# Mamba layers as a pipeline of token halves: the end of one item and the preparation of the next are issued between the scan chunks of the one in the middle

## The reference

```python
def rmsnorm(x, w, eps=1e-05):
    return x * jax.lax.rsqrt(jnp.mean(x * x, axis=-1, keepdims=True) + eps) * w
def mamba_block(x, ...):
    xm, res = jnp.split(x @ in_w.T + in_b, 2, axis=-1)
    xm = jax.nn.silu(causal_depthwise_conv(xm, conv_w) + conv_b)      # 4 taps over tokens
    x_dbl = xm @ xp_w.T
    delta = jax.nn.softplus(x_dbl[..., :64] @ dt_w.T + dt_b)
    Bm, Cm = x_dbl[..., 64:80], x_dbl[..., 80:]
    def step(h, ins):                                                 # scan over tokens
        d_t, B_t, C_t, u_t = ins
        h = h * jnp.exp(d_t[:, :, None] * A) + (d_t * u_t)[:, :, None] * B_t[:, None, :]
        return (h, jnp.einsum('bds,bs->bd', h, C_t))
    y = (ys + xm * D_ssm) * jax.nn.silu(res)
    return y @ out_w.T + out_b
x1 = x + mb(rmsnorm(x, norm1_w)); out2 = memory_attend(mb(rmsnorm(x1, norm2_w))); return x1 + out2
```

## Time and profile before

| | |
|---|---|
| median of three runs | 3658.72 us |
| the profiled execution, its time / span | 3660.78 us / 3659.0 us |
| busy: PE / DVE / ACT / POOL | 2742.5 / 2217.9 / 1904.8 / 1665.2 us |
| share of the span | 75% / 61% / 52% / 46% |
| granted TensorE clock, mean | 0.90 |
| chain that ended last: PE / POOL / DVE / issue / ACT | 41% / 30% / 11% / 8% / 7% |
| the four batches / what follows them | 38 to 2765 us / 2765 to 3659 us |

### The profile page before, as it was taken

The page is one execution under the profiler, slowest core; times in us unless marked ns, Lnnn a source line. Parts: engine busy times, 40 slices in busy tenths (PEclk is TensorE's granted clock), DMA queues, the critical chain, the costliest instruction groups (busy, mean ns, idle before and its releaser), DMA issues.

```text
span 3659.0 us, 44328 instructions
## 1 busy us (share of the span) xinstructions
PE 2742.5 (75%) x15274; PEld 2050.4 (56%) x15275; DVE 2217.9 (61%) x2787; ACT 1904.8 (52%) x3028; POOL 1665.2 (46%) x1723
## 2 busy tenths in 40 slices
PE   5787688877777896687688867777895299999910
PEld 2674576547647754674676547647754166666600
DVE  4894893468668645894893468678643033333347
ACT  5785781378678525785781378678531011111100
POOL 2792791039639602792791039639602501000060
PEclk9898899889989998898899889989996599999955
DMA  5110120001001100110110001001102212111031
GB/s 197 43 51 1 41 64 1 12 18 52 25 18 50 38 1 13 44 50 1 44 61 1 12 18 53 24 18 53 35 1 102 81 62 90 62 63 62 33 93 47
DMA packets 91235, 158.84 MB, mean 43 GB/s; under 512 B 14130, under 2 KB 39986, under 8 KB 91058
## 3 DMA queue, kind: packets, MB, share of 16 engines
q1 hardware_dynamic: 72338, 106.80, 9.4%
q0 software_dynamic: 15392, 47.99, 3.6%
q10 hardware_dynamic: 3328, 1.76, 0.2%
HBM read 118.36 MB, written 38.14 MB: 43 GB/s over the span
## 4 chain that ended last, share of the span: by engine, by line
PE 41%; POOL 30%; DVE 11%; issue 8%; ACT 7%; DMA 2%; another core or an unknown queue 1%; DVEq 0%; POOLq 0%; SPq 0%; ACTq 0%
POOL arena L597 25%; PE psD L926 13%; PE psD L1237 7%; PE psA L926 6%; POOL arena L582 4%; PE psD L1114 2%; PE psA L1089 2%; PE psD L1135 2%; DVE arena L1351 2%; PE psA L973 2%; PE psA L1228 1%; DVE arena L1349 1%; PE psA L920 1%; ACT arena L779 1%; DVE arena L1338 1%
## 5 line engine op out<-in xcount | busy, mean ns | idle before, releaser
L597 POOL TENSOR_TENSOR arena<-arena 128x512 f32<-128x512 f32 x1024 | 1091.2, 1092 | 10.7 <-POOL carry L593 0.5
L1012 PE MATMUL psD<-ident,arena 128*128 128x128 f32 x4096 | 651.6, 286 | 274.6 <-ACT arena L779 209.9
L1012 PEld LDWEIGHTS psD<-ident,arena 128*128 128x128 f32 x4096 | 479.1, 146 | 374.0 <-ACT arena L779 273.5
L786 ACT ACTIVATE arena<-arena,negA 128x512 f32<-128x512 f32 x1024 | 662.1, 712 | 12.2 <-DVE arena L1363 11.4
L1363 DVE TENSOR_TENSOR_SCAN arena<-arena,psD 128x512 f32<-128x512 f32 x512 | 581.7, 1200 | 137.8 <-PE psA L1032 81.4
L1032 PE MATMUL psA<-ident,arena 128*128 128x128 f32 x4096 | 617.7, 274 | 19.0 <-POOL arena L597 18.7
L1363 DVE TENSOR_TENSOR_SCAN arena<-arena,carry,psD 128x512 f32<-128x512 f32 x512 | 602.4, 1255 | 37.0 <-PE psA L1032 37.0
L779 ACT ACTIVATE arena<-arena,bc 128x512 f32<-128x512 f32 x768 | 498.0, 712 | 87.4 <-PE psD L1012 86.3
L1032 PEld LDWEIGHTS psA<-ident,arena 128*128 128x128 f32 x4096 | 479.1, 142 | 32.3 <-POOL arena L597 32.3
L926 PE MATMUL psD<-arena 128*128 128x512 f32 (+4 forms) x776 | 336.9, 569 | 43.5 <-POOL strip L545 28.7
L883 ACT ACTIVATE in_w_sb<-in_w_sb 128x512 f32<-128x512 f32 x140 | 88.1, 630 | 457.6 <-DVE in_w_sb L1559 457.6
(11 more groups left out here) (202 smaller groups left out, 3527.6 us busy)
## 6 DMA issues: line engine op xcount, KB each, us to landing
arena<-c_dram SPq DMA_DIRECT2D x256, 256.0 KB, 3.2
arena<-in_W POOLq DMA_DIRECT2D x16, 1024.0 KB, 7.5
xs_dram<-zeros SPq DMA_DIRECT2D x40, 256.0 KB, 6.5
arena<-xs_dram SPq DMA_DIRECT2D x71, 128.0 KB
ys_dram<-arena POOLq DMA_DIRECT2D x70, 128.0 KB, 2.0
arena<-in_x SPq DMA_DIRECT2D x4, 1024.0 KB, 7.0
arena<-in_b POOLq DMA_DIRECT2D x8, 512.0 KB, 7.9
out<-arena SPq DMA_DIRECT2D x4, 1024.0 KB
```

The lines of the kernel that those rows point to most:

```text
L597: pool.tensor_tensor(h_ring[:, r % H_SLOTS, :], h_ring[:, r % H_SLOTS, :], c_rows[:, (half * NS + n) % C_SLOTS, :], ALU.mult).then_inc(c_w ...
L786: act.activation(da_ring[:, r % DA_SLOTS, :], dt[:, f, half * HALF:(half + 1) * HALF], ACT.Exp, scale=negA[:, f, n:n + 1]).then_inc(da_rea ...
L1012: mm = pe.transpose(psD[:, r % RING, j * P:(j + 1) * P], g[:, (r // KI) % 2, j, f * P:(f + 1) * P], ident[:, :])
```

## The change

A layer is no longer prepared for 1024 tokens at once. The four items of a batch are layer 0 first half, layer 0 second half, layer 1 first half, layer 1 second half. They form one scan run of 256 chunks a batch (`RUN = ITEMS * CHUNKS`). Every engine walks the steps c = -64 .. 256 + 19. `when(c)` gives the place r within a window of 64 chunks, and the items k (ending), s (being scanned) and p (being prepared). A table of constants says at which r each piece is issued; the piece comes after that step's regular work on its queue. The run's chunks are as wide as before.

- Two banks of psD take fills, the other two take all side work, under new semaphores (`bg_full`, `bg_by_act`, `bg_by_dve`). The decay ring has six slots instead of eight.
- Softplus runs block by block, and its functions alternate with the decays. The root is exp(-0.5 ln(mean + eps)) on ACT; before it was Sqrt on ACT and a reciprocal on DVE. POOL normalises. All tests for small exponentials are on POOL.
- The convolution carries its last three tokens from the first to the second half of a layer (`pads`).
- The output bias is added to x in place by POOL, layer 0 adds into xin, and x is read again from DRAM into base at the end of the batch for the final sum.
- The first part of x2 is read back after the last layer norm of the last batch; before, it was read after layer 0 of that batch.
- Zeros are written to DRAM in pieces twice as wide.

The diff, cut to its core. The constants and the two helpers:

```diff
-        RUN = 2 * CHUNKS
-        DA_SLOTS = H_SLOTS = 8
-        C_SLOTS = 4
+        ITEMS = 4
+        RUN = ITEMS * CHUNKS
+        TAIL = 20
+        DA_SLOTS, H_SLOTS, C_SLOTS = 6, 8, 4
+        FILL_BANKS = 2
         FILL_AHEAD, SUM_AFTER, DECAY_AHEAD, WEIGH_AFTER = 2, 6, 4, 4
...
+        TURN = [8, 10, 12, 14]
+        MO = [10, 12, 14, 16]
+        XNT = [22, 23]
+        IN = [25, 27, 29, 31]
+        GATE = [26, 28, 30, 32]
+        XD = [38]
+        BCT = [40]
+        Z = [41, 42, 43, 44]
+        UT = [50, 51, 52, 53]
+        KEEP_Y = 6
+        PADS, XB = 2, 1
+        SQUARE = [MO[j] + 2 for j in range(JT)]
+        RMS, NORM = 19, 20
+        SILU = 36
+        SOFT = [z + 2 for z in Z]
...
+        def when(c):
+            s, r = divmod(c, CHUNKS)
+            items = [q if 0 <= q < ITEMS else None for q in (s - 1, s, s + 1)]
+            return (r, *items)
```

SP:

```diff
+                for v in range(ITEMS * NS):
+                    q, n = divmod(v, NS)
+                    i = b * ITEMS + q
+                    if n == NS - 2 and q + 1 < ITEMS:
+                        store_c(i + 1)
...
+                sp.wait_ge(bg_by_dve, taken("turn", b * ITEMS + ITEMS - 1, JT - 1))
+                sp.dma_start(base, x[b].rearrange("(t p) d -> p t d", p=P)).then_inc(x_again, 16)
...
+            sp.wait_ge(ln_done, B * 2 * TT)
             sp.dma_start(x2[:, 0:TT, :], x2_dram[0:TT].rearrange("t p d -> p t d")).then_inc(x2_first, 16)
```

POOL:

```diff
+                def normalise(i):
...
+                    pool.wait_ge(inverse, 2 * (i + 1))
+                    for j in range(JT):
+                        pool.tensor_scalar(xn[:, j, :], xin[:, (i % 2) * JT + j, :],
+                                           inv_rms[:, 1, j:j + 1], 1.0, ALU.mult, ALU.mult).then_inc(normed, 1)
+                def soften(i, f):
+                    n = i * KI + f
+                    pool.wait_ge(soft_exp, n + 1)
+                    if n >= 2:
+                        pool.wait_ge(replaced, n - 1)
+                    pool.tensor_scalar(is_small[:, f % 2, :], soft_e[:, f, :], SMALL_E, None, ALU.is_lt)\
+                        .then_inc(small_found, 1)
+                    pool.wait_ge(slope_ready, n + 1)
+                    pool.tensor_tensor(series[:, f % 2, :], series[:, f % 2, :], soft_e[:, f, :], ALU.mult)\
+                        .then_inc(cubic_step, 1)
...
+                for c in range(-CHUNKS, RUN + TAIL):
+                    r, k, s, p = when(c)
+                    if (c + 6) % KI == 0 and 0 <= (c + 6) // KI < ITEMS * NS:
+                        spread_b((c + 6) // KI)
+                    if 0 <= c - WEIGH_AFTER < RUN:
+                        weigh_c(c - WEIGH_AFTER)
+                    if s is not None and s < 2 and r == XB:
+                        add_bias(i0 + s)
+                    if p is not None and r == NORM:
+                        normalise(i0 + p)
+                    if p is not None and r - 1 in SOFT:
+                        soften(i0 + p, SOFT.index(r - 1))
```

ACT:

```diff
+                def find_rms(i):
+                    act.wait_ge(squares, JT * (i + 1))
+                    act.activation(inv_rms[:, 0, :], mean_sq[:, :], ACT.Ln, scale=1.0 / D, bias=eps_sb[:, 0:1]).then_inc(inverse, 1)
+                    if i > 0:
+                        act.wait_ge(normed, JT * i)
+                    act.wait_ge(inverse, 2 * i + 1)
+                    act.activation(inv_rms[:, 1, :], inv_rms[:, 0, :], ACT.Exp, scale=-0.5).then_inc(inverse, 1)
...
+                def decline(i, f):
+                    n = i * KI + f
+                    act.wait_ge(bg_by_dve, taken("z", i, f))
+                    act.activation(soft_e[:, f, :], dt[:, i % 2, f, :], ACT.Abs).then_inc(soft_abs, 1)
+                    act.wait_ge(soft_abs, n + 1)
+                    act.activation(soft_e[:, f, :], soft_e[:, f, :], ACT.Exp, scale=-1.0).then_inc(soft_exp, 1)
+                def slope(i, f):
+                    n = i * KI + f
+                    act.wait_ge(soft_exp, n + 1)
+                    if n >= 2:
+                        act.wait_ge(replaced, n - 1)
+                    act.activation(series[:, f % 2, :], soft_e[:, f, :], ACT.Copy, scale=1.0 / 3.0, bias=-0.5)\
                        .then_inc(slope_ready, 1)
...
+                    act.activation(soft_ln[:, f % 2, :], soft_e[:, f, :], ACT.Ln, bias=1.0).then_inc(soft_log, 1)
...
+                for c in range(-CHUNKS, RUN + TAIL):
+                    r, k, s, p = when(c)
+                    if 0 <= c + DECAY_AHEAD < RUN:
+                        decay(c + DECAY_AHEAD)
...
+                    if p is not None and r - 1 in IN:
+                        f = IN.index(r - 1)
+                        if f == 0:
+                            act.wait_ge(pads_zero, i0 + p + 1)
+                        bg_drain("in", i0 + p, f, pre[:, f, TAPS - 1:TAPS - 1 + HALF], ACT.Identity, bias=in_b_sb[:, f:f + 1])
+                        tap0(i0 + p, f)
...
+                    if p is not None and r == SILU:
+                        silu_conv(i0 + p)
+                    if s is not None and r == SILU:
+                        silu_gate(i0 + s)
...
+                    if p is not None and r in SOFT:
+                        decline(i0 + p, SOFT.index(r))
+                    if p is not None and r - 1 in SOFT:
+                        slope(i0 + p, SOFT.index(r - 1))
```

PE:

```diff
+                def fill(c):
+                    if c % KI == 0:
+                        pe.wait_ge(b_by_act, JS * (b * ITEMS * NS + c // KI + 1))
+                        pe.wait_ge(b_by_pool, b * ITEMS * NS + c // KI + 1)
+                    if c >= FILL_BANKS:
+                        pe.wait_ge(scanned, b * RUN + c - FILL_BANKS + 1)
...
+                for c in range(-CHUNKS, RUN + TAIL):
+                    r, k, s, p = when(c)
+                    if 0 <= c + FILL_AHEAD < RUN:
+                        fill(c + FILL_AHEAD)
+                    if 0 <= c - SUM_AFTER < RUN:
+                        add_y(c - SUM_AFTER)
+                    if k is not None and r in MO:
+                        leave(i0 + k, MO.index(r))
+                    if k is not None and r in TURN:
+                        turn_y(i0 + k, TURN.index(r))
```

The rest of PE's loop issues `turn_y`, `turn_xn`, `project_in` for `IN` and `GATE`, `project_x`, `turn_bc`, `project_dt` and `turn_u` at their places. DVE:

```diff
+                for c in range(-CHUNKS, RUN + TAIL):
+                    r, k, s, p = when(c)
+                    if 0 <= c < RUN:
+                        scan(c)
...
+                        gate_y(i0 + k, TURN.index(r - 1))
+                    if p is not None:
+                        for f in range(KI):
+                            for tap in range(1, TAPS):
+                                if r == IN[f] + 1 + tap:
+                                    convolve(i0 + p, f, tap)
+                        if r - 1 in Z:
+                            add_dt_b(i0 + p, Z.index(r - 1))
+                        for f in range(KI):
+                            if r == SOFT[f] + 2:
+                                expand(i0 + p, f)
+                            if r == SOFT[f] + 3:
+                                replace(i0 + p, f)
+                            if r == SOFT[f] + 4:
+                                finish_dt(i0 + p, f)
+                            if r == SOFT[f] + 5:
+                                times_u(i0 + p, f)
```

More of the change, by code:

```diff
@@ new lines, in decoder_layer @@
+        GATE = [26, 28, 30, 32]
[9 more added lines that the diff above has]
+        SOFT = [z + 2 for z in Z]
+        conv_order = [(f, tap) for r in range(CHUNKS) for f in range(KI) for tap in range(1, TAPS) if r == IN[f] + 1 + tap]
+        STAGES = (("mo", MO, -1, "dve"), ("turn", TURN, -1, "dve"), ("xnT", XNT, 1, "act"), ("in", IN, 1, "act"),
+                  ("gate", GATE, 0, "act"), ("xd", XD, 1, "act"), ("bcT", BCT, 1, "act"), ("z", Z, 1, "dve"),
+                  ("uT", UT, 1, "act"))
```

816 lines of the change are left out of this document (378 added, 438 removed).

## The result

The changed kernel takes 3890.1 us (median of 4 runs, 3878.0 to 3906.5), the kernel before 3656.5 in the same comparison (3632.0 to 3663.4): ratio **1.065, 95% interval 1.060 to 1.071**. It is 6.5% slower. The profiled execution, the slowest of the four, took 3906.5 us for a span of 3905.0, 246 more than before.

The account below looks back on a forecast made before the run. It took the scan loop as bound by POOL (100%) and VectorE (90 to 100%); 654 us added against 620 removed gave +34, 3692 against the median, likeliest 3690, own range 3620 to 3760, with large rivals 3545 to 3815.

Parts of the forecast that it names:

- Zeroing in wider pieces, other semaphores and the layout: nothing: Side edits to zero writes, semaphores and array layout: no added time, hidden by the first load of weights.
- Turning, gating and projecting y: Steps 8 to 17: VectorE's gate products, sums and small PE waits add 5 us in each of 12 items, +60.
- The PE work beside it, eight projections of two products at 0.45 ... stay below VectorE's time: Convolution, steps 25 to 35: PE's projections and the eight drains of 0.68 stay below VectorE's time.
- The term, +12: Convolution, steps 25 to 35: VectorE's scans, taps and waits add 12 us an item, +144, bounds 6 and 19.
- Rings at nothing: Two fill banks instead of four, six decay slots instead of eight: counted as no added time.
- too short a ring: Slower rival: PE late in each chunk with the shorter rings, 0.1 us each, 100 us; 3790, chance 0.05.
- Softplus, +31: Softplus and Silu, steps 36 to 51: 52 us where 17 chunks took 21, +31 an item, +372, bounds 27 and 36.
- The lock at 0.4 to 1.0: Convolution taps: VectorE waits on POOL's SBUF work, 0.4 us after a scan, 1.0 for a pair's second, 6.6 together.
- the two rivals built on it: VectorE and POOL sharing SBUF: lock hardly paid, 3545, chance 0.27; or lock in full, 3815, chance 0.22.
- the term of step 3: Convolution, steps 25 to 35: 27.4 us instead of 13.8, less 1.1 counted elsewhere, +12 an item.
- Gains outside the run: Per batch outside the scan run: first preparation 33 us less, end of batch 13 us less.
- if PE ends the waits of the scans: Sign named beforehand that the forecast is wrong: the scans' waits are ended by PE.

Follow-up runs that it names:

- c_lag: `a_place` with VectorE taking PE's turned and output blocks two steps after PE's piece instead of one, later stages moved two steps; 1.020 of the kernel before.
- c_best: Changed kernel with ring of states moved 8 bytes, softplus logarithms in pairs, and VectorE two steps behind PE, all together; 1.0027 of the kernel before.
- d_gate: `c_best` with the four gate projections moved from the steps between the input projections to steps 19, 21, 23, 26; 1.016 of the kernel before.
- b_da: Kernel before with the ring of decays, which also holds the softplus exponentials, 8 bytes on; ratio 0.9997.
- f_both: `c_best` without two of three convolution taps and one product of each projection, output wrong; steps 28 to 35 of the third item fall to 18.2 us.
- p_4: Kernel before with C rows 4 bytes later; 3811 us, where the kernel before took 3630.
- p_16: Changed kernel with the ring of states 16 bytes on; 3878 us, where the kernel before took 3630.
- a_place: Changed kernel with the ring of states, and the gated block behind it, moved 8 bytes on; 1.042 of the kernel before.

## Why the prediction was wrong

It said 3690 (3545 to 3815) with 0.43 for slower; it was 3890. The direction had its chance, the size lay outside. Two terms put at nothing (1 and 4) and two that were too small (2 and 3) made the difference:

1. **"Zeroing in wider pieces, other semaphores and the layout: nothing"** failed. The layout put states and C rows at the same place modulo 16 bytes: +0.18 us for each of 1024 C products, 23.8 us a batch, 95 in all. It was neither in the sum nor among the rivals. The earlier trace rows gave the price of a chunk, and I took it over without asking if it hung on addresses. With it mended the time was 3802, inside the range only just.
2. **"Turning, gating and projecting y": +5 an item, where "VectorE ... waits a little for PE"** failed. Steps 8 to 19 of item 2 take 26.5 us against 15.3, +11. I had set VectorE's own work down and not what stands behind its wait: its next scans, then PE's fills, which have only two banks. `c_lag` gives back 20.4 a batch.
3. **"The PE work beside it, eight projections of two products at 0.45 ... stay below VectorE's time"** was mis-sized. The row with 48 matmuls covers 12 jobs of 2 products; each fp32 product is two instructions. A job is 1.78 us, not 0.9 (1.88 in the trace after). PE then needs 20.8 us where VectorE needs about as much. The term, +12, came to +13, +18 and +13 in the three items (steps 24 to 35, 15.3 undisturbed), and in the crowded steps of `c_best` PE and VectorE were about equal, not VectorE alone.
4. **Rings at nothing** failed: 7.8 us a batch in the kernel before, 31 in all. The rival *too short a ring* had a chance of 0.05 and over twice the price in all; its 0.1 a chunk showed in the second halves of a layer alone.
5. **Softplus, +31** held: steps 36 to 51 take 51.9, 48.5 and 49.8 us in the three items, where 52 was forecast, nearly all of the excess in steps 40 to 51 (+32, +27 and +30 over 15.3). So did its parts: ScalarE full up to step 47 and VectorE behind it (rows above), and 1.28 us a load with nothing beside it (52 us for 56 loads fewer). Placement and rings are in these figures too; with the placement mended they are 47.9, 49.1 and 47.9, which is within the term's bounds of 27 to 36. The term's "17 chunks" are 16 steps, and POOL's tests take 1.69 us, not "at most 1.38": neither decided. The drain of 1.38 us that the Trainium skill ("ScalarE: Activation LUTs", section What ACT_TABLE_LOAD costs) adds is not seen: in the timeline the Ln starts 1.29 after the load's start, and the load 0.02 after the end of what ran before it. VectorE's waits for POOL's cubic stand there too (66 us in 64).
6. **The lock at 0.4 to 1.0** was sized too high: the taps' mean is 0.98 against 1.2 forecast, the median 0.75, single ones 1.5. Over the shortest tap of 0.72 that is 0.26 of waiting, about half of the 0.55 in the sum. The rule of the Trainium skill on the shared port ("SBUF — State Buffer", section SBUF: two separate sides) agrees with `d_gate`'s taps of 0.97 to 1.50 us beside others of 0.72, but neither of the two rivals built on it decided. This error spared time, so that the term of step 3 is off by more than its total shows.
7. **Gains outside the run**: -46 a batch forecast (33 + 13), -30.0 measured; 7.3 of the difference came back with the placement, 7.8 more with the other two mends.

Of the signs named beforehand the unbroken run and the loads (192) came. The fourth item took 103 us instead of 90, the others 134, 150 and 141 instead of 130 to 135, and a batch's first scan came 57 us after normalisation instead of 49. One sign of being wrong came as well, "if PE ends the waits of the scans": 168 of the 256 us that the scans wait are ended by PE's sums, 50 more than before. What the mended version shows is the base of all this: an item with a preparation still takes 130 us, VectorE busy 112 and ScalarE 110 of it,

```profile
212.94:342.84 129.90, 106.71 (x668) 82.01 (x668) 111.62 (x105) 110.14 (x179) 100.53 (x95) 0.92 0.13 34
```

against 79 to 84 for 64 chunks in the kernel before. Overlap gave back the chains' idle time and no more, because the scan loop had left no room on POOL, little on VectorE and a tenth on ScalarE.

## What to carry over

Before work is put between the steps of a full loop, add up each engine's work per item, with every queue's order: a wait costs what stands behind it, not the waiting engine's own time. Where two engines have about the same load in a stretch, lightening one gives little (VectorE alone nothing here, PE alone 0.5 to 1.9 us of 3), so test both at once before discarding them. When arrays move, compare the shortest instance of each old operation in both traces first: it is the quickest sign that an operation itself, not its surroundings, has changed.

## What was not expected of the hardware

- A POOL product of two fp32 operands in SBUF (128x512) takes 1.08 us if they start 8 bytes apart modulo 16, and 1.25 if they start 0 or 4 bytes apart; 128x1024: 2.00 and 2.35 (shortest instances). The first pair is seen in six kernels, the second in two. VectorE's scan (1.23) does not depend on where the ring of decays starts. Two sums of 2048 columns on POOL, operands at the same place modulo 16, took 4.50 and 4.52 us in the kernel before. An estimate that goes on in a line from 512 over 1024 columns gives 4.53 for the slow placement and 3.83 for the fast one, so these sums fit the slow one, and moving one of their operands by 8 bytes may save time too; no run tried it.

```profile
L562 POOL TENSOR_TENSOR arena<-arena x4: 4496/4497/4498, 308.7 to 2364.0; 128x2048 f32<-128x2048 f32 x4
```

- The last part of the profiled executions comes in two lengths, 1045 to 1057 or 1015 to 1032 us with the same output: from the last gather's start to the end it is 78 to 82 us in some and 45 to 53 in others. It goes mostly with the chip and not with the edit: on the chips of the first comparisons and of the last (`b_da`, `f_both`) the longer one, on the three of all others, `p_4` and `p_16` included, the shorter one, where the kernel before takes 3629 to 3630 us instead of 3652 to 3657. `a_place` alone (53 us) stands apart from its neighbours, and its own four times fall into two pairs, 3793 and 3811. What differs is open. It is why batches, not totals, were compared above.
